# State space stage of a decoder kernel: y's first value from one factor per head, roots a step later, low weight halves in odd steps, x transposed ahead

## The reference, cut to what matters

```python
zxbcdt = x @ W_in.T                     # z, xBC, dt_raw
xBC = _causal_conv_silu(xBC, conv_w)    # xs (512), B (128), C (128)
dt = jax.nn.softplus(dt_raw + dt_bias)
a = dt * A; cum = jnp.cumsum(a, axis=2)
Lmat = exp(cum[i] - cum[j]) for j <= i
M = CB * Lmat * dt[j]                   # CB = C @ B.T
Yd = einsum('bcijh,bcjhp->bcihp', M, xs)
y = (Yd + Yoff) + D * xs
yz = y * silu(z)
yn = yz * rsqrt(mean(yz * yz) + EPS) * norm_w
return yn @ W_out.T
```

## Time and profile before

| | |
|---|---|
| median of 3 runs | 2156.69 us (2154.9 to 2158.75) |
| profiled execution: time | 2156.69 us |
| profiled execution: span, first to last instruction | 2154.9 us |
| busy: PE / DVE / ACT / POOL | 1976.9 / 1631.3 / 1378.5 / 1253.1 us |
| mean granted TensorE clock | 0.979 |
| state space stage | about 863 to 1258 us of the span |

### The profile page before, as it was taken

How to read it: one execution, slowest core, us unless ns; L and a number is a source line. 1 busy time by engine, 2 the same in 40 slices (tenths; PEclk the granted TensorE clock), 3 DMA queues, 4 the chain that set the end, 5 groups by cost and what they waited for, 6 DMA issues and landing times.

```text
span 2154.9 us, 34806 instructions
## 1 busy us (share of the span) xinstructions
PE 1976.9 (92%) x9518; PEld 1275.5 (59%) x9620; DVE 1631.3 (76%) x3836; ACT 1378.5 (64%) x5262; POOL 1253.1 (58%) x1524
## 2 busy tenths in 40 slices
PE   7979999999999998798988858999999999999996
PEld 5636666666666665454444425666666666666664
DVE  7845677677767677789889735788888888887887
ACT  3555666666666665366563227777777777777774
POOL 0154444545454452487877834777777777777774
PEclk9999999999999999999999969999999999999999
DMA  6000000000000002100000010000000000000000
GB/s 227 1 18 6 3 3 3 2 5 2 2 2 2 2 0 85 69 11 30 20 20 10 0 61 28 4 4 6 6 7 5 6 5 6 8 6 6 3 3 8
DMA packets 30241, 37.61 MB, mean 17 GB/s; under 512 B 3472, under 2 KB 24464, under 8 KB 29456
## 3 DMA queue, kind: packets, MB, share of 16 engines
q1 hardware_dynamic: 30096, 36.11, 4.9%
HBM read 34.01 MB, written 2.10 MB: 17 GB/s over the span
## 4 chain that ended last, share of the span: by engine, by line
PE 57%; DVE 18%; POOL 9%; issue 8%; ACT 7%; DMA 0%; DVEq 0%; POOLq 0%; SPq 0%; ACTq 0%
PE xa_pS L755 5%; PE xa_pJB L736 5%; PE fa_pJB L1987 5%; PE xa_pO L830 5%; PE xa_pY L867 5%; PE xa_pJA L736 4%; PE fa_pS L2069 3%; PE fa_pO L2012 3%; PE fa_pY L2026 3%; PE fa_pJA L1967 2%; POOL ssm_y L1380 2%; PE fa_pH L2118 2%; PE xa_pP L747 2%; POOL fa_rs L1917 2%; PE fa_pH L2085 2%
## 5 line engine op out<-in xcount | busy, mean ns | idle before, releaser
L2144 ACT ACTIVATE fa_qT<-fa_pH,all_fa_head_vec 128x512 f32<-128x512 f32 x128 | 99.6, 778 | 176.3 <-PE fa_pH L2118 176.3
L1917 POOL TENSOR_TENSOR fa_rs<-fa_rs,all_minus_half 128x4 f32<-128x4 f32 x192 | 197.6, 1029 | 15.0
L1380 POOL TENSOR_TENSOR ssm_y<-ssm_y,ssm_term 128x512 f32<-128x512 f32 x112 | 150.4, 1343 | 76.9 <-DVE ssm_term L1681 66.4
L2153 ACT ACTIVATE fa_pS<-fa_pS,fa_nb 128x128 f32<-128x128 f32 x512 | 183.2, 394 | 6.7 <-issue 6.7
L1914 POOL TENSOR_TENSOR fa_rs<-fa_ms,all_eps5w 128x4 f32<-128x4 f32 x192 | 44.3, 231 | 227.6 <-ACT fa_q_junk L2137 126.5
L2069 PEld LDWEIGHTS fa_pS<-fa_kT,fa_qT 128*128 128x128 f32 x1024 | 124.2, 191 | 65.5 <-ACT fa_qT L2144 58.5
L1942 POOL TENSOR_TENSOR fa_cat<-fa_ov,fa_om 128x512 bf16<-128x512 f32 x125 | 150.5, 1204 | 5.1
L2069 PE MATMUL fa_pS<-fa_kT,fa_qT 128*128 128x128 f32 x1024 | 148.1, 288 | 2.8 <-ACT fa_qT L2144 0.9
L1933 POOL TENSOR_TENSOR fa_ov<-fa_ob,fa_om 128x512 f32<-128x512 bf16 x125 | 144.4, 1155 | 0.9 <-DVE fa_om L2285 0.9
L682 POOL TENSOR_TENSOR xa_rs<-xa_ms,all_eps 128x4 f32<-128x4 f32 (+1 forms) x65 | 13.2, 204 | 223.1 <-ACT xa_junk L906 223.1
L924 ACT ACTIVATE xa_pr<-xa_pS,xa_nb,xa_rs 128x256 f32<-128x256 f32 x256 | 142.5, 568 | 0.2
...
## 6 DMA issues: line engine op xcount, KB each, us to landing
...
```

Of the source, the lines that this page charges most:

```text
L1380: pool.tensor_tensor(y[:, side, :], y[:, side, :], term[:, in_turn(side, l), :], ALU.add)\
L1917: pool.tensor_tensor(rs[:, j % 2, cols], rs[:, j % 2, cols], env.mhalf[:, cols], ALU.pow)\
L2153: last = act.activation(four(pS[j % 2])[:, i, :], four(pS[j % 2])[:, i, :], ACT.Exp, bias=nb[:, j % 2, i:i + 1], accum_out=rsum[:, j % 2, ...
```

## The change

y0 becomes xs times one factor per head and token. The factor `own`, 64 columns, is `dt` times `cbd` plus D, made by VectorE once `cbd` is there, in the step before its use; y0 is then one product on VectorE that reads xs and `own`. POOL's skip goes. As y0 now reads xs, ACT writes the next xs only when y0 is done.

POOL's root of the variance moves from after the last addition to after the third addition of the next step. VectorE does terms 5 and 6 in a row; normalising, residual and statistics come after both. Low halves are taken in odd steps only, one chunk before term 4 and one after it. xT gets two buffers; TensorE transposes x for the next pair before the sixth tap of an odd step, and ACT copies it before xs. The products for dt come after z in an even step and always use bank pE, once ACT has read the previous decays from it; the waits that tied them to `norm.summed` and the projection to `dt_biased` go.

```diff
@@ -1196,7 +1196,7 @@
         return w_tap[:, slot // 2, slot % 2, at:at + 2 * H].rearrange("p (b h) -> p b h", b=2)
 
     dt_in, e_abs, one_p, log_p, part, dt, a = [small(n) for n in range(7)]
-    xT = sb("xT", [P, 2, KT, PAD + P])
+    xT = sb("xT", [P, 2, 2, KT, PAD + P])
     dec = sb("dec", [P, 2, LEVELS, 2, H])
     xdt = sb("xdt", [P, HID])
     xd = sb("xd", [P, 2, LEVELS, HID])
@@ -1204,7 +1204,7 @@
     cbd = sb("cbd", [P, 1])
     junk = sb("junk", [P, P])
     junk2 = sb("junk2", [P, HID], BF16)
-    skip = sb("skip", [P, HID])
+    own = sb("own", [P, H])
     ms = sb("ms", [P, 1])
     rms = sb("rms", [P, 1])
     pZ, pX, pC, pE = ps("pZ"), ps("pX"), ps("pC"), ps("pE")
@@ -1214,7 +1214,7 @@
     names = ("xT_ps", "xT_in", "dt_ps", "bc_ps", "xs_ps", "z_ps", "dt_biased", "minus_abs", "e_done",
              "one_p_done", "log_done", "part_min", "part_inv", "part_log", "one_is", "part_sum",
              "dt_done", "a_done", "bc_in", "xs_in", "z_in", "cb_ps", "dec_ps", "dec_in", "dec_late", "cb_done",
-             "xdt_done", "xd_vector", "cbd_done", "skip_done", "y0_done", "gated", "squared",
+             "xdt_done", "xd_vector", "cbd_done", "own_done", "y0_done", "gated", "squared",
              "ms_eps", "rms_done", "yT_ps", "yT_in", "o_ps", "bc_scaled")
     SHIFTS = ((1, 0), (1, 1), (2, 0), (2, 1), (3, 0), (3, 1))
     bc_added = sem("bc_added", len(SHIFTS))
@@ -1307,12 +1307,12 @@
         if b == 0:
             act.wait_ge(pad_in, 1)
         act.wait_ge(s["xT_ps"], of_pair(b + 1))
-        act.activation(xT[:, :, :, PAD:PAD + P], pZ[:, :].rearrange("p (b k c) -> p b k c", b=2, k=KT),
+        act.activation(xT[:, pair(b + 1) % 2, :, :, PAD:PAD + P], pZ[:, :].rearrange("p (b k c) -> p b k c", b=2, k=KT),
                        ACT.Copy).then_inc(s["xT_in"], 1)
 
     def dt_bank(b):
 
-        return pO[:, D:D + 2 * H] if b > 2 else pE[:, 0:2 * H]
+        return pE[:, 0:2 * H]
 
     def span_bank(m, l):
 
@@ -1381,18 +1381,15 @@
                         .then_inc(y_added, 1)
                     if l == 1 and back:
                         pool_rms(m - 1)
-                    if l == 6 and back:
-                        norm.pool_rstd(pool, m - 1, 0)
+                    if l == 2 and m > 2:
+                        norm.pool_rstd(pool, m - 2, 0)
             elif back:
+                norm.pool_rstd(pool, m - 2, 0)
                 pool_rms(m - 1)
                 norm.pool_rstd(pool, m - 1, 0)
             if first:
                 for j in range(4):
                     tail(0, j)
-            if front:
-                pool.wait_ge(s["xs_in"], now(m + 1, 0))
-                pool.tensor_tensor(heads(skip[:]), heads(xs[:]), per_head(d_skip[:]), ALU.mult)\
-                    .then_inc(s["skip_done"], 1)
             if front:
                 pool.wait_ge(s["xdt_done"], now(m + 1, 0))
                 pool.wait_ge(s["dec_late"], of_pair(m + 1))
@@ -1434,7 +1431,7 @@
             def tap(n):
 
                 t, k = n // KT, n % KT
-                return pe.matmul(pX[:, :], xT[:, m % 2, k, t:t + P], w_tap[:, t, k, 0:HID],
+                return pe.matmul(pX[:, :], xT[:, pair(m + 1) % 2, m % 2, k, t:t + P], w_tap[:, t, k, 0:HID],
                                  start=(n == 0), stop=(n == TAPS * KT - 1))
 
             levels = iter(range(LEVELS))
@@ -1455,8 +1452,6 @@
             def project_out(b):
                 pe.wait_ge(s["yT_in"], now(b, 0))
                 pe.wait_ge(norm.summed, now(b, 0) - 1)
-                if b + 1 < B and b % 2:
-                    pe.wait_ge(s["dt_biased"], of_pair(b + 2))
                 for k in range(HID // P):
                     last = pe.matmul(pO[:, 0:D], yT[:, k * P:(k + 1) * P], w_out[:, k, :],
                                      start=(k == 0), stop=(k == HID // P - 1))
@@ -1464,27 +1459,27 @@
 
             if front:
                 pe.wait_ge(s["xT_in"], of_pair(m + 1))
-                if m > 1:
-                    pe.wait_ge(norm.summed, now(m - 2, 0))
-                for n in range(0 if m % 2 else 2):
-                    for k in range(KT):
-                        last = pe.matmul(dt_bank(m + 1)[:, n * H:(n + 1) * H], xT[:, n, k, PAD:PAD + P],
-                                         w_dt[:, k, :], start=(k == 0), stop=(k == KT - 1))
-                    if n == 1:
-                        last.then_inc(s["dt_ps"], 1)
                 pe.wait_ge(s["cbd_done"], now(m, 0))
                 for half in range(2):
                     for k in range(KT):
                         last = pe.matmul(pC[:, half * N:(half + 1) * N],
                                          w_tap[:, 0, k, HID + half * N:HID + (half + 1) * N],
-                                         xT[:, m % 2, k, PAD:PAD + P], start=(k == 0), stop=(k == KT - 1))
+                                         xT[:, pair(m + 1) % 2, m % 2, k, PAD:PAD + P], start=(k == 0), stop=(k == KT - 1))
                 last.then_inc(s["bc_ps"], 1)
                 if m % 2:
                     pe.wait_ge(s["z_in"], now(m, 0))
                 for k in range(KT):
-                    last = pe.matmul(pZ[:, :], xT[:, m % 2, k, PAD:PAD + P], w_z[:, k, :],
+                    last = pe.matmul(pZ[:, :], xT[:, pair(m + 1) % 2, m % 2, k, PAD:PAD + P], w_z[:, k, :],
                                      start=(k == 0), stop=(k == KT - 1))
                 last.then_inc(s["z_ps"], 1)
+                if m % 2 == 0:
+                    pe.wait_ge(s["dec_in"], of_pair(m))
+                    for n in range(2):
+                        for k in range(KT):
+                            last = pe.matmul(dt_bank(m + 1)[:, n * H:(n + 1) * H],
+                                             xT[:, pair(m + 1) % 2, n, k, PAD:PAD + P],
+                                             w_dt[:, k, :], start=(k == 0), stop=(k == KT - 1))
+                    last.then_inc(s["dt_ps"], 1)
                 if first:
                     tail(0, 0)
                     tail(0, 1)
@@ -1506,12 +1501,12 @@
                     project_out(m - 1)
                 if first and n == 4:
                     tail(0, 2)
+                if front and n == 6 and m + 1 < B and m % 2:
+                    transpose_x(m + 1)
                 if front and n >= early:
                     last = tap(n)
             if front:
                 last.then_inc(s["xs_ps"], 1)
-                if m + 1 < B and m % 2:
-                    transpose_x(m + 1)
                 if m % 2 == 0:
                     pe.wait_ge(s["a_done"], of_pair(m + 1))
                     pe.wait_ge(s["dec_late"], of_pair(m))
@@ -1592,10 +1587,11 @@
                 tail(0, 2)
                 tail(0, 3)
             if front:
-                act.wait_ge(s["xs_ps"], now(m + 1, 0))
-                act.activation(xs[:], pX[:, :], ACT.Silu).then_inc(s["xs_in"], 1)
                 if m + 1 < B and m % 2:
                     copy_x(act, m + 1)
+                act.wait_ge(s["xs_ps"], now(m + 1, 0))
+                act.wait_ge(s["y0_done"], now(m, 0))
+                act.activation(xs[:], pX[:, :], ACT.Silu).then_inc(s["xs_in"], 1)
                 if m % 2 == 0:
                     p = pair(m + 1)
                     act.wait_ge(s["dec_ps"], now(p, 0, 2, 0))
@@ -1690,10 +1686,9 @@
                     .then_inc(s["gated"], 1)
             terms(0, 1)
             if attend:
-                dve.wait_ge(s["skip_done"], now(m, 0))
-                dve.wait_ge(s["cbd_done"], now(m, 0))
-                dve.scalar_tensor_tensor(out=y[:, side, :], in0=xdt[:], scalar=cbd[:], in1=skip[:],
-                                         op0=ALU.mult, op1=ALU.add).then_inc(s["y0_done"], 1)
+                dve.wait_ge(s["own_done"], now(m, 0))
+                dve.tensor_tensor(heads(y[:, side, :]), heads(xs[:]), per_head(own[:]), ALU.mult)\
+                    .then_inc(s["y0_done"], 1)
             if paired:
                 softplus(m + 1)
             if front:
@@ -1710,8 +1705,11 @@
                 tail(0, 2)
             if m == 1:
                 scale_out_weights()
+            if m % 2:
+                chunk_low(m - 4)
             terms(4)
-            chunk_low(m - 3)
+            if m % 2:
+                chunk_low(m - 3)
             if front:
                 dve.wait_ge(s["cb_ps"], now(m + 1, 0))
                 dve.tensor_tensor(cb[:, 1 - side], pC[:, 0:P].unsqueeze(1).to_broadcast([P, LEVELS, P]),
@@ -1719,10 +1717,15 @@
                 dve.scalar_tensor_tensor(out=junk[:], in0=pC[:, 0:P], scalar=1.0,
                                          in1=env.ident[:], op0=ALU.mult, op1=ALU.mult,
                                          accum_out=cbd[:]).then_inc(s["cbd_done"], 1)
+                dve.wait_ge(s["cbd_done"], now(m + 1, 0))
+                dve.wait_ge(s["dt_done"], of_pair(m + 1))
+                dve.wait_ge(s["y0_done"], now(m, 0))
+                dve.scalar_tensor_tensor(out=own[:], in0=dt[:, m % 2], scalar=cbd[:], in1=d_skip[:],
```

(4 more changed lines are left out.)

## The result

The changed kernel takes 2137.85 us (median of four runs, 2136.56 to 2138.07) against 2156.68 for the kernel before, measured beside it: a ratio of 0.9913, interval 0.990 to 0.9926. It is 0.87% faster, and 5.4 us faster than forecast. The profiled execution has a span of 2136.1 us, 18.8 less than before.

What follows compares the result with a forecast made beforehand. The prediction took a path through POOL where two steps meet and VectorE in their middle to bound the kernel. Its terms summed to −13.4 us: 2154.9 − 13.4 + 1.8 = 2143.3 us, range 2134 to 2152.

Steps and rivals of the forecast that it cites:

- Seams: Between two steps, from L1270's end to the first addition: 4.1 us in the odd step, both kinds gaining 0.95 us.
- Terms 5 and 6 together: End of each step: L1270 takes 2.29 us instead of 3.24, 0.95 gained; L112 waits for POOL, 0.4 lost.
- Root: POOL's root now stands between the third and fourth addition of a step: 0.3 us lost, ends 0 and 0.55.
- Even steps: Steps without low halves take 20.6 us, 3.06 less, as TensorE and ACT hold them until the decays are there.
- Step 14: Step with POOL's one-off addition for the next stage's weights: held by TensorE after that, it gains 0.95 twice, −1.9 us.
- Step 0: First step of the state-space stage: dt's products follow z, so VectorE gets dt later, 1.1 us lost.
- Low halves in odd steps: VectorE in the odd step: the second pair of low halves costs 1.53 us, ends 0.1 and 3.1.
- First rival: Odd step: less collision, the second pair of low halves costs 0.3 us instead of 1.53; 2136 us, chance 0.14.
- Second rival: Odd step: its room is an illusion, the second pair of low halves costs 3.1 us; 2153 us, chance 0.10.
- Fourth: Odd step: VectorE comes second at every meeting, and the clock falls in each even step; slower, 2165 us, chance 0.05.
- Fifth: Between steps: waiting takes the skip's place, so 0.3 us is gained rather than 0.95; 2150 us, chance 0.09.
- Third rival, the clock: Even steps: TensorE idles before the levels, its clock falls to 0.50, each loses 1.6 us; 2151 us, chance 0.12.

Runs made afterwards that it cites:

- the filler: The changed kernel with two matmuls more in each even step, ahead of the levels, whose result nothing reads: 2136.08 us.
- y0 and root: The kernel before with y0 from the own factor on VectorE, no skip on POOL, and POOL's root moved a step later: 2150.04 us, ratio 0.9971.
- low halves each step: The changed kernel with one chunk of low halves in every step, after term 4, as before: 2148.25 us, ratio 0.9955.

## Why the prediction was right, and where its steps were off

The time, 2137.85 us, lies in the stated range of 2134 to 2152, but below the 2139 to 2147 that had half of the chance. The span was forecast to change by −13.4 and changed by −18.8 us. By kinds of step, from the ends of L1270 on VectorE:

| steps | predicted | measured |
|---|---|---|
| 0 | +1.1 | +1.07 |
| 1 | −0.75 | −0.77 |
| 3 | −0.6 | −0.47 |
| 4, 6, 8, 10, 12 | −15.3 | −14.1 |
| 5, 7, 9, 11, 13 | +3.0 | +0.1 |
| 14 | −1.9 | −3.64 |
| 15 | +0.6 | −0.75 |
| 16, 17 | +0.5 | −0.3 |

The steps of the table sum to −18.9. In these two traces the stretch ahead of the stage is 1.35 us longer and the one behind it 1.35 us shorter; that the two cancel is chance.

- **Seams.** Right. Predicted 4.1 us in the odd and 4.5 in the even step from L1270's end to the first addition; measured 4.08 and 4.44. The root's share in the chain, the largest of rows 2, was mostly somebody else's wait: alone it was worth nothing. The prediction had priced it through the seam as a whole, with skip and root together 0.95. That was right for their sum, of which the skip carries 0.8. Two sums on the way there do not close, to little effect: three inputs of 1.03 and a collision of 0.45 make 3.54, not 3.60, and 2.7, 0.6 and 0.7 make 4.0, not 4.1.
- **Terms 5 and 6 together.** Right in mechanism: L1270 takes 2.29 us in all sixteen steps. The price on L112 was undersized, 0.4 against 0.64. I had taken its longest row before (0.78 of rows 6); now it starts behind term 6 while the addition of term 5 has 0.9 us to go (1080.67 against 1081.58).
- **Root** in the middle: 0.3 taken, 0.38 and 0.49 measured. **Own factor**: 0.25 taken, 0.285 measured, 0.3 on the path.
- **Even steps.** 20.6 predicted from step 2 (rows 1), 20.47 measured in three of five. So the claim was right that TensorE and ACT hold that step once VectorE's 2.4 us are gone: L1270 at its end waits 0.19 us for ACT's decays, and with two taps taken out of TensorE's way the step still falls only to 20.33.

```profile
1062.45 2.29 DVE L1270 TENSOR_TENSOR ssm_xd<-ssm_xdt,ssm_dec 128x2048 f32<-128x2048 f32 x1 [0.19 <-ACT ssm_dec L1598]
```

- **Step 14.** Wrong. The prediction put the low halves at nothing there, as TensorE would hold the step, and gave no row for that. With low halves in each step it takes 25.88 us, without 23.57: they are worth 2.3 us there as well.
- **Step 0.** The size, 1.1 against 1.07, is right by luck in part: all of it was laid to dt, which carries 0.68; the own factor, which the prediction left out of this step, carries the rest.
- **Low halves in odd steps**, the widest term, was mis-sized: 1.53 taken, 0.61 measured. I took the price of a pair behind the hole, 2.86, and subtracted the hole of 1.33. But term 4 is written while POOL still adds term 3, so its delay costs nothing, and the pair in the hole is paid only by what it collides with, 0.45 in the root and 0.14 in an addition. This is the mechanism of the first rival (less collision, 0.3); its size lies between it and the forecast. In step 15 the same term gives most of the miss. In the odd steps a second error hid 0.4 of this one: all other terms together gained only 0.59 us (21.42 to 20.83) of the 0.95 predicted.
- **First rival**, less collision: nearest in time (2136), though its odd step of 20.8 us did not come (21.44); part of the match is step 14, which it did not touch. **Second rival**, room in odd steps an illusion: fell, with 0.61 against its 3.1. **Fourth**, slower: fell; it had each L1661 at 1.76 us, and their mean is 1.375. **Fifth**: fell at the seams.
- **Third rival, the clock**: came true in part, in two of five even steps, 0.9 us each against the 1.6 priced. It is in the result, and the filler shows that it is the clock. The prediction's 1.6 was half of 3.1 us at low clock; of 3.4 us measured, half of which would be 1.7, the step lost only 0.97, so that TensorE was not last in all of it.

The Trainium skill, page "SBUF — State Buffer", section "Who interferes with whom", says that a VectorE instruction with two SBUF inputs and a GpSimd instruction that reads SBUF contend for one shared port pair, which is locked exclusively. The changed kernel shows it at its plainest in step 14, where y's first value, 0.68 us alone, meets POOL's addition of the mean to weights:

```profile
1177.68 3.31 DVE L1690 TENSOR_TENSOR ssm_y<-ssm_xs,ssm_own 128x512 f32<-128x512 f32 x1
```
```profile
1176.84 3.60 POOL L1402 TENSOR_TENSOR all_shared_weights<-all_shared_weights 128x2048 f32<-128x2048 f32 x1
```

It ends at 1180.99, 0.55 us after POOL's at 1180.44. The trace agrees with the rule. L112, which waits in the same way (0.40 against 1.05 us), reads one SBUF tensor and two columns of one number per partition: the prediction's "wherever both read two tensors of SBUF" is too narrow.

Left open: why the clock falls in steps 6 and 12 and not in 8 and 10, whose wait before the levels is the same 2.25 us; so it was in all three profiles whose steady stretch is the changed kernel's. Two other variants had falls in other steps. With low halves in each step the waits are shorter, 1.66 us, and the clock fell in steps 6 and 8, which took 23.36 and 23.22 us instead of 22.65; with terms 5 and 6 apart they are 2.6 us, and it fell in steps 6 and 10. Here is step 6 of the first of these, with a window behind its wait:

```profile
1003.47 1.10 PE L1428 MATMUL ssm_pL<-ssm_xd,ssm_cb 128*128 128x512 f32 x1 [1.66 <-issue]
```
```profile
1003.60:1006.90 3.30, 3.30 (x4) 1.16 (x5) 2.92 (x3) 0.31 (x1) 3.26 (x3) 0.50 0.00 0
```

So the length of the wait alone does not decide it.

Not split further: the 0.66 us a pair between "y0 and root" and "low halves each step" holds terms 5 and 6, the second buffer of xT and the place of dt; the terms explain 0.5 of it (42.40 against 41.91 a pair, measured on the changed kernel), and the others were not tried alone.
